# Reordering three engines inside one attention step of a conv, attention and expert kernel

## The reference, cut to what matters

```python
x = x + _L0_conv_ref(_gn(x), L0_conv_conv_w, L0_conv_conv_b)
t = _to_tokens(x)
t = t + _L1_attn_ref(_ln_t(t), L1_attn_wq, L1_attn_wk, L1_attn_wv)      # causal softmax attention
t = t + _L1_ffn_ref(_ln_t(t), L1_ffn_Wg, L1_ffn_bg, ...)                 # gate = xf @ Wg.T + bg; top 1 of 8
```

## Time and profile before

| what | us |
|---|---|
| median of 3 runs (303.17 to 304.46) | 303.44 |
| time of the profiled execution | 305.84 |
| its span | 304.0 |
| PE busy | 226.3 |
| DVE busy | 176.0 |
| ACT busy | 124.3 |
| POOL busy | 93.6 |

### The profile page before, as it was taken

The page is one execution under the profiler, slowest core; times in us unless marked ns, Lnnn a source line. Parts: engine busy times, 40 slices in busy tenths (PEclk is TensorE's granted clock), DMA queues, the critical chain, the costliest instruction groups (busy, mean ns, idle before and its releaser), DMA issues.

```text
span 304.0 us, 5067 instructions
## 1 busy us (share of the span) xinstructions
PE 226.3 (74%) x1354; PEld 205.9 (68%) x1355; DVE 176.0 (58%) x561; ACT 124.3 (41%) x255; POOL 93.6 (31%) x102
## 2 busy tenths in 40 slices
PE   1486699897418966887876742079999999999981
PEld 1376598786408866877765632058989898998971
DVE  2253643640348364876787566736767677676750
ACT  1513134621134766896776203114433333443330
POOL 2211020100000065388786855501221222221222
PEclk9999999999655878997999555559999999999997
DMA  7976721221000005234543301022322000000000
GB/s 232 365 246 207 223 70 43 80 62 51 0 2 1 0 0 181 81 123 182 206 155 114 156 26 54 27 68 74 86 70 58 26 14 17 7 22 26 17 20 0
DMA packets 15713, 25.78 MB, mean 85 GB/s; under 512 B 3879, under 2 KB 12643, under 8 KB 14672
## 3 DMA queue, kind: packets, MB, share of 16 engines
q1 hardware_dynamic: 13824, 22.40, 23.0%
q0 software_dynamic: 1872, 3.18, 3.0%
HBM read 19.50 MB, written 6.76 MB: 86 GB/s over the span
## 4 chain that ended last, share of the span: by engine, by line
PE 52%; DVE 19%; POOL 9%; issue 8%; ACT 6%; DMA 3%; POOLq 0%; DVEq 0%; SPq 0%; ACTq 0%
PE bank L1209 6%; PE bank L1185 4%; PE bank L958 4%; PE bank L960 4%; PE bank L959 4%; PE bank L962 4%; PE bank L961 4%; PE bank L972 3%; POOL wall L383 3%; PE bank L1210 3%; POOL wall L385 2%; PE bank L953 2%; DVE gst L617 2%; PE bank L1200 2%; PE bank L980 2%
## 5 line engine op out<-in xcount | busy, mean ns | idle before, releaser
L411 POOL DMA_INDIRECT out_rows<-yo,rows x23 | 22.4, 975 | 84.2 <-DVE yo L927 84.2
L383 POOL TENSOR_TENSOR wall<-stage,wall 128x940 fp32r<-128x940 f32 x8 | 17.5, 2190 | 56.4 <-ACT wall L500 47.6
L1209 PE MATMUL bank<-wall,HH 128*128 x92 | 29.4, 374 | 1.5 <-DVE HL L907 1.5
L912 DVE TENSOR_TENSOR gh<-gh,bank 128x470 f32<-128x470 f32 x23 | 14.8, 645 | 22.1 <-PE bank L962 21.2
L577 ACT ACTIVATE HH<-bank 128x512 fp32r<-128x512 f32 x23 | 13.8, 600 | 31.1 <-PE bank L1185 31.1
L1210 PE MATMUL bank<-wall,HL 128*128 x92 | 23.1, 251 | 0.0
L365 POOL DMA_INDIRECT token_rows<-rows,posi x16 | 19.0, 1188 | 9.7 <-issue 7.4
L958 PE MATMUL bank<-wall,FH 128*128 x46 | 19.7, 429 | 1.0 <-DVE FL L915 1.0
L907 DVE TENSOR_TENSOR HL<-bank,HH 128x512 fp32r<-128x512 f32 x23 | 15.9, 692 | 7.3 <-ACT HH L577 6.1
L583 ACT ACTIVATE FH<-bank 128x256 fp32r<-128x256 f32 x23 | 8.9, 385 | 24.6 <-PE bank L1200 23.2
L580 ACT ACTIVATE gh<-bank 128x470 f32<-128x470 f32 x23 | 13.0, 565 | 13.5 <-PE bank L962 13.5
(11 more groups left out here) (218 smaller groups left out, 723.5 us busy)
## 6 DMA issues: line engine op xcount, KB each, us to landing
stage<-in_w_all SPq DMA_DIRECT2D x8, 1324.0 KB, 6.4
rows<-token_rows SPq DMA_DIRECT2D x23, 98.0 KB
near_rows<-gram SPq DMA_DIRECT2D x8, 243.0 KB, 2.6
xcm<-in_x_cm SPq DMA_DIRECT2D x2, 768.0 KB, 9.4
rows<-in_x_tm SPq DMA_DIRECT2D x1, 1536.0 KB, 14.4
token_rows<-emptyt SPq DMA_DIRECT2D x9, 98.0 KB, 5.6
taps_sb<-near_rows SPq DMA_DIRECT2D x8, 103.0 KB, 2.1
small_sb<-in_small SPq DMA_DIRECT2D x1, 704.0 KB, 15.4
```

The costliest lines, as they stand in the source:

```text
L383: nc.gpsimd.tensor_tensor(w[:, W12:2 * W12], stage[:, par, 0:W12], w[:, 0:W12].bitcast(F32), ALU.subtract)
L411: pool.indirect_dma_start(out=out, out_offset=bass.IndirectOffsetOnAxis(ap=rows[:, j, C + 2:C + 3].bitcast(U32), axis=0), in_=yo[:, par], ...
L1209: nc.tensor.matmul(dst[:, 0:2 * C], HH[:, 1 - par, k], w(0, P, c0, c0 + 2 * C), start=(k == 0), stop=False)
```

## The change

Four pieces of work are put at other places of their engine's list; no arithmetic is added or removed.

On DVE, the six gate operations of image t-3 stand ahead of `xn2` of image t-2 (before: behind it). `XL`, which a step computed for image t near its start, is computed for image t+1 at the end of step t, ahead of the positions; `XL` of image 0 comes before step 0. On PE, the gate of image t-3 stands right behind the scores, ahead of U; and V of image t stands ahead of the transposes of the probabilities of image t-1.

```diff
@@ -754,9 +754,16 @@
                 nc.vector.scalar_tensor_tensor(out=ln1[:, lo:hi, 0], in0=ln1[:, lo:hi, 0], scalar=-1.0, in1=y,
                                                op0=ALU.mult, op1=ALU.mult).then_inc(ln1_ready, 1)
 
+            def low_tokens(t, par):
+
+                ve.wait_ge(xh_ready, t + 1 + AHEAD)
+                nc.vector.tensor_tensor(XL[:, par].rearrange("p t x -> p (t x)"), bank[0][:],
+                                        XH[:, par].rearrange("p t x -> p (t x)").bitcast(F32), ALU.subtract).then_inc(xl_ready, 1)
+
             ve.wait_ge(conv_taken, IMAGES)
             token_stats(0, QUARTER)
             token_factors(0, QUARTER, 1)
+            low_tokens(0, 0)
 
             def step(t, par, weights=True):
                 done = [0]
@@ -771,10 +778,6 @@
 
                     ve.wait_ge(o_ready, t - 1 + AHEAD)
                     link(nc.vector.reciprocal(rsum[:], ssum[:]))
-                if on(t, 0):
-                    ve.wait_ge(xh_ready, t + 1 + AHEAD)
-                    nc.vector.tensor_tensor(XL[:, par].rearrange("p t x -> p (t x)"), bank[0][:],
-                                            XH[:, par].rearrange("p t x -> p (t x)").bitcast(F32), ALU.subtract).then_inc(xl_ready, 1)
                 if isinstance(t, int) and t == 0:
                     token_stats(QUARTER, TILES)
                 if on(t, 1):
@@ -806,14 +809,6 @@
                     ve.wait_ge(uh_ready, t + 1 + AHEAD)
                     nc.vector.tensor_tensor(uAl[:, par], bank[1][:, 0:PIX], UH[:, par, 0].bitcast(F32), ALU.subtract)
                     nc.vector.tensor_tensor(UH[CB:P, par, 1], bank[1][CB:P, PIX:2 * PIX], UH[CB:P, par, 1].bitcast(F32), ALU.subtract).then_inc(ul_ready, 1)
-                if on(t, 2):
-
-                    ve.wait_ge(rs_ready, t - 1 + AHEAD)
-                    ve.wait_ge(t2t_ready, t - 2 + AHEAD)
-                    for h in range(HALVES):
-                        row = rows[:, bass.ds(2 * t + (h - 4), 1), 0:C].rearrange("p a c -> p (a c)")
-                        ins = nc.vector.tensor_scalar(xn2[:, h], row, ln2[:, h, 0:1], ln2[:, h, 1:2], ALU.subtract, ALU.mult)
-                    ins.then_inc(xn2_ready, 1)
                 if on(t, 3):
 
                     ve.wait_ge(g_ready, t - 2 + AHEAD)
@@ -825,11 +820,23 @@
                     link(nc.vector.tensor_tensor(lg[:], lg[:], desc, ALU.mult))
                     link(nc.vector.tensor_reduce(gmx[:], lg[:], AX_X, ALU.max))
                     nc.vector.tensor_tensor(oh[:], lg[:], gmx[:].rearrange("p (h a) -> p h a", a=1).to_broadcast(wide), ALU.is_equal).then_inc(oh_ready, 1)
+                if on(t, 2):
+
+                    ve.wait_ge(rs_ready, t - 1 + AHEAD)
+                    ve.wait_ge(t2t_ready, t - 2 + AHEAD)
+                    for h in range(HALVES):
+                        row = rows[:, bass.ds(2 * t + (h - 4), 1), 0:C].rearrange("p a c -> p (a c)")
+                        ins = nc.vector.tensor_scalar(xn2[:, h], row, ln2[:, h, 0:1], ln2[:, h, 1:2], ALU.subtract, ALU.mult)
+                    ins.then_inc(xn2_ready, 1)
                 if weights:
 
                     ve.wait_ge(wall_hi, t - 1)
                     w = wall[CB:P, bass.ds(t - 2, 1), 2 * W12:3 * W12].rearrange("p a c -> p (a c)")
                     nc.vector.tensor_tensor(w, stage[CB:P, par, W12:2 * W12], w.bitcast(F32), ALU.subtract).then_inc(wall_q, 1)
+                if isinstance(t, int) and t == 0:
+                    token_factors(QUARTER, TILES, 2)
+                if on(t, -1):
+                    low_tokens(t + 1, 1 - par)
                 if on(t, 3):
 
                     ve.wait_ge(pf_ready, t - 2 + AHEAD)
@@ -846,8 +853,6 @@
 
             for t in range(3):
                 step(t, t % 2, t > 1)
-                if t == 0:
-                    token_factors(QUARTER, TILES, 2)
             with ve.Fori(1, IMAGES // 2 - 1) as i:
                 for u in range(2):
                     step(2 * i + (u + 1), 1 - u)
@@ -1079,6 +1084,16 @@
                         nc.tensor.matmul(dst, UH[:, old, 1, q], xh_b, start=False, stop=False)
                         mm = nc.tensor.matmul(dst, UH[:, old, 1, q], xl_b, start=False, stop=True)
                     mm.then_inc(s_ready, 1)
+                if on(t, 3):
+
+                    pe.wait_ge(x2_copied, t - 2 + AHEAD)
+                    pe.wait_ge(pos_ready, t - 3 + AHEAD)
+                    wg = c2("wg")
+                    for h in range(HALVES):
+                        dst = bank[7][:, EXPERTS * h:EXPERTS * (h + 1)]
+                        nc.tensor.matmul(dst, x2T[:, 0, P * h:P * (h + 1)], wg[:, 0:EXPERTS], start=True, stop=False)
+                        mm = nc.tensor.matmul(dst, x2T[:, 1, P * h:P * (h + 1)], wg[:, EXPERTS:2 * EXPERTS], start=False, stop=True)
+                    mm.then_inc(g_ready, 1)
                 if on(t, 0):
 
                     pe.wait_ge(xl_ready, t + 1 + AHEAD)
@@ -1093,30 +1108,20 @@
                         nc.tensor.matmul(dst, mH[:, q], XH[:, par, 1], start=False, stop=False)
                         mm = nc.tensor.matmul(dst, mH[:, q], XL[:, par, 1], start=False, stop=True)
                     mm.then_inc(u_ready, 1)
+                if on(t, 0):
+
+                    pe.wait_ge(v_copied, t + AHEAD)
+                    for h in range(HALVES):
+                        q = slice(P * h, P * (h + 1))
+                        mm = products(bank[2][:, C * h:C * (h + 1)], XH[:, par, 0, q], XL[:, par, 0, q], XH[:, par, 1, q], XL[:, par, 1, q],
+                                      vwH[:, 0:C], vwL[:], vwH[:, C:2 * C])
+                    mm.then_inc(v_ready, 1)
                 if on(t, 1):
                     pe.wait_ge(exp_ready, t + AHEAD)
                     pe.wait_ge(pt_copied, t - 1 + AHEAD)
                     for k in range(3):
                         mm = nc.tensor.transpose(bank[4][:, P * k:P * (k + 1)], Pr[:, P * k:P * (k + 1)], ident)
                     mm.then_inc(pt_ready, 1)
-                if on(t, 0):
-
-                    pe.wait_ge(v_copied, t + AHEAD)
-                    for h in range(HALVES):
-                        q = slice(P * h, P * (h + 1))
-                        mm = products(bank[2][:, C * h:C * (h + 1)], XH[:, par, 0, q], XL[:, par, 0, q], XH[:, par, 1, q], XL[:, par, 1, q],
-                                      vwH[:, 0:C], vwL[:], vwH[:, C:2 * C])
-                    mm.then_inc(v_ready, 1)
-                if on(t, 3):
-
-                    pe.wait_ge(x2_copied, t - 2 + AHEAD)
-                    pe.wait_ge(pos_ready, t - 3 + AHEAD)
-                    wg = c2("wg")
-                    for h in range(HALVES):
-                        dst = bank[7][:, EXPERTS * h:EXPERTS * (h + 1)]
-                        nc.tensor.matmul(dst, x2T[:, 0, P * h:P * (h + 1)], wg[:, 0:EXPERTS], start=True, stop=False)
-                        mm = nc.tensor.matmul(dst, x2T[:, 1, P * h:P * (h + 1)], wg[:, EXPERTS:2 * EXPERTS], start=False, stop=True)
-                    mm.then_inc(g_ready, 1)
                 if on(t, 1):
 
                     pe.wait_ge(pt_copied, t + AHEAD)
```

More of the change, by code:

```diff
@@ L1095, in step @@
                     mm.then_inc(u_ready, 1)
[L1096 to L1101, removed]
                 if on(t, 0):
@@ L1109, in step @@
                     mm.then_inc(v_ready, 1)
-                if on(t, 3):
-                    pe.wait_ge(x2_copied, t - 2 + AHEAD)
-                    pe.wait_ge(pos_ready, t - 3 + AHEAD)
-                    wg = c2("wg")
-                    for h in range(HALVES):
-                        dst = bank[7][:, EXPERTS * h:EXPERTS * (h + 1)]
-                        nc.tensor.matmul(dst, x2T[:, 0, P * h:P * (h + 1)], wg[:, 0:EXPERTS], start=True, stop=False)
-                        mm = nc.tensor.matmul(dst, x2T[:, 1, P * h:P * (h + 1)], wg[:, EXPERTS:2 * EXPERTS], start=False, stop=True)
-                    mm.then_inc(g_ready, 1)
+                if on(t, 1):
+                    pe.wait_ge(exp_ready, t + AHEAD)
+                    pe.wait_ge(pt_copied, t - 1 + AHEAD)
+                    for k in range(3):
+                        mm = nc.tensor.transpose(bank[4][:, P * k:P * (k + 1)], Pr[:, P * k:P * (k + 1)], ident)
+                    mm.then_inc(pt_ready, 1)
                 if on(t, 1):
```

## The result

The changed kernel took 321.04 us in the median of six runs (316.98 to 323.14), against 303.72 us before on the same chip; the ratio is 1.047 with a 95% interval of 1.041 to 1.053, so some 318 us for a kernel of 303.7. It is slower, by about what was forecast (318.0, from 311 to 325).

What follows compares the result with a forecast made beforehand. Order and waits between engines, not work, were taken to bound the attention stage. Terms 1.1 + 2.6 + 2.1 + 10.1 + 0.7 - 2.3 + 0.25 = +14.6 us on 303.44 gave 318.0 us, range 311 to 325.

Steps and rivals of the forecast that it cites:

- the loop: Attention stage: positions, gate, U, V, transposes, ACT's list to `XH`, `XL`, positions follow one another; 13.1 us a step.
- V in steps 1 to 3, `XL` ahead in step 3: V delays `PT`: +1.1 us in step 1, +2.6 in steps 2 and 3; `XL` delays step 3's positions: +2.1.
- steps 4 to 6: From step 3's positions to step 6's: three loops of 13.1 us, 39.3 against 29.2, +10.1 us.
- step 7: No image 8, so no `XL`; positions to positions 9.9 us against 9.20, +0.7.
- step 8: Weights' transfer in time, -1.0 us; gate operations inside the wait for POOL, -1.3; together -2.3.
- step 9: Gate operations take 1.48 us in a 1.23 us wait for POOL: +0.25 us.
- The length of the half clock: PE at half clock for 3.3 us at the start of each such step, putting `PT` 5.39 us behind the positions.
- rival B: Half clock holds through the PE part of each step: loop 14.5 us, +20.9 in all, 324.3 us; chance 0.16.
- rival A: Half clock doesn't come or goes at once: loop 11.65 us, +8.9 in all, 312.3 us; chance 0.14.
- Rival E: DVE's gate operations and POOL hold each other up, costing +1.2 us in step 8: 319.2 us; chance 0.08.
- Rival C: POOL's loop sets the pace at 8.8 us a step, bounded by POOL's own 9 or so: 299 us; chance 0.03.
- D: The order costs nothing, the waits only change names: 303.4 us; chance 0.04.

Runs made afterwards that it cites:

- the filler runs: Changed kernel plus 20 unread matmuls of 128 columns, behind the scores from step 1 on or ahead of the gate in steps 3 to 7: 317.7 and 316.6 us.
- first filler run: Changed kernel plus 20 matmuls of 128 columns, read by nothing, behind the scores of each step from 1 on: 317.7 us, ratio 1.043.

## Why the prediction was right, point by point

The stated mechanism was the one that ran. One term, the loop, was too small for the profiled execution, by 3.3 us of 13.4. That the ratio comes out at 318 to the tenth is luck: the profile lost 17.3 us where 14.6 were forecast, the median of all six runs is 321.0, and the table shows terms that are off in either direction.

| term | predicted | in the profile |
|---|---|---|
| start of step 1 | 0 | -0.4 |
| V in steps 1 to 3, `XL` ahead in step 3 | +5.8 | +5.3 |
| steps 4 to 6 | +10.1 | +13.4 |
| step 7 | +0.7 | +0.7 |
| step 8 | -2.3 | -1.7 |
| step 9 | +0.25 | 0.0 |
| sum | +14.6 | +17.3 |

- *One loop instead of two side by side.* Shown by the rows of step 4, and by experiments: put back `XL`, or PE's gate, or only the gate's reason to wait, and 10.5 to 13.9 us go from three steps that had lost 13.4. Neither `XL` nor the gate makes this loop alone. The gate alone is a gain of 2.5 us over the same stretch, V alone a loss of 1.65, `XL` alone, by another loop through the maxima and exponentials, a loss of 8.15. That adds up to 7.3 us; together they cost 13.4.
- *V ahead of the transposes.* Right in sign, and near in the sum of steps 1 to 3 (5.3 us with `XL`'s 1.9, where I had 5.8), but not step by step: from one `XH` to the next, step 1 cost 0.1 us (I had 1.1), step 2 1.2, step 3 2.1 (I had 1.3 each). In step 1 the clock was 1.00, where it was 0.82 before; step 3 ran at 0.57. Alone it costs 2.7 us by P(3); inside the loop 6.65 us over three steps. It isn't a fixed price, though: with `XL` ahead and the gate free it costs 0.8 over the three.
- *The length of the half clock* is the mis-sized term. I took 3.3 us at half in each step from step 2 of the kernel before. It held for about 6.8 us. In step 4 gate, U and V ran at half throughout: 1.70 + 2.28 + 2.08 us, where the gate alone had been put at 1.50; in steps 5 and 6 the clock had fallen before the gate began, and rose before V's end. `PT` came 7.03, 6.59 and 6.35 us behind the positions in the three steps, where I had 5.39 and for all at half 6.81. That is rival B in the loop, and 13.4 against its 14.4. In step 2 the half clock was near what I took; in step 3 it stood from 118.5 to 128.8, about 10 us.
- *PE's idle time* was the reason given for the half clock, 4.4 to 5.5 us of it. The clock fell, but PE stood only 1.95 us ahead of the gate in step 4, and 3.57 and 3.61 in steps 5 and 6. In step 4 the half clock held just as long as in the other two, so the length of the idle time doesn't tell how long the half clock holds.
- *At full clock* the loop is 11.46 to 11.48 us, from the filler runs; I had worked out 11.65 (rival A). So rival A has the size about right and a condition that doesn't hold here.
- *ACT's list from `PT` to `XH`*: 5.85 predicted, 5.84 measured.
- *Step 7* 9.86 us against 9.89. *Step 8*: the transfer was in time (ACT's L495 of step 7 no longer waits), and POOL's weights began 0.34 us behind the positions; I had 0.08. Behind `xn2` the gate operations' removal saved 1.0 us (192.99 - 190.02 = 2.97 against 175.65 - 171.69 = 3.96 in the earlier trace rows), where I took 1.3.
- *Rival E*, in part: L819 reads two SBUF tensors and took 1.19 us on 16 columns, ending at 189.02 with POOL's L385 (188.99), as L882 of the earlier trace rows, done at 193.94, ended with POOL's L385 there (193.90). The three gate operations behind it still ended before `xn2` began at 190.02, so it cost next to nothing. The Trainium skill, page "SBUF — State Buffer", section "SBUF: two separate sides", says that such an operation waits out the whole GpSimd instruction if that one began first and reads SBUF; the trace agrees, with 1.19 us behind L385's start at 187.19, where the same line took 0.17 in step 4.
- *Rival C and D* fell: neither POOL's loop nor the old waits set the pace. But C's number, 299 us, is what the gate edits give when `XL` and V stay where they were; that the numbers agree is luck, since C had `XL` ahead.

What stays open: why one run takes 317 us and another 322, and what in PE's activity lets the clock fall in one step and not in the next, with the same matmuls in it.

## What to carry to other kernels

Before an operation is put ahead of a signal on an engine that works through a fixed list, write down what waits for that signal, and follow it round. An edit that is good alone (the gate, 1.6% faster) can, together with another, join two loops that ran side by side, and their parts then follow one another. Try parts of a reordering singly; here one of three was worth 1.6%, and the other two cost 2.1% and 3.0%. A wait that a shared buffer imposes can be removed by another buffer whose order is already kept by existing waits.

## What the runs showed of the hardware

In the profiled execution the granted clock of TensorE made nearly half of the loss, by an estimate from the filler runs: 42.63 - 3 x 11.47 = 8.2 us of 17.3. 20 additional matmuls in the idle time, 2.35 us in all, made a step shorter by some 2.7 us in three of six cases, though PE had more to do. In the other three the mean clock was still 0.73 or 0.87.

The length of PE's idle time did not tell whether the clock would fall. In step 3 of the changed kernel it fell at 118.5, where the longest idle time since 109 had been 0.81 us, and came back at 128.8. In the first filler run it stayed at 1.00 after an idle time of 0.69 us ahead of the gate of step 4, and fell 2.2 us after the end of one of 0.76 in step 5. A late start of PE is therefore not shown to be what lowers the clock; what is shown is that a stretch at the half clock makes `PT`, and with it the positions and PE's next start, later.
